# Keys and values of the last key tile as whole fp32 matmuls instead of three matmuls on parts

## What is computed

```python
# layer 0
memory_proj = einsum('bme,de->bmd', ctx, W_mem)
attn = softmax(einsum('bnd,bmd->bnm', x, memory_proj) / sqrt(256))
memory_context = einsum('bnm,bmd->bnd', attn, memory_proj)
gate = sigmoid(concat([x, memory_context]) @ W_gate.T + b_gate)
x = rmsnorm(x + gate * memory_context) * norm_w
# layer 1: 16 heads of 64
q = layernorm(x) @ Wq / 8
k, v = split(ctx @ Wkv)                 # (4, 512, 1024) each
sim = where(mask, q @ k.T, min)
x = x + tanh(attn_gate) * (softmax(sim) @ v) @ Wo
x = x + tanh(ff_gate) * gelu(layernorm(x) @ W1) @ W2
```

## Time and profile before

| | us |
|---|---|
| median of 3 runs | 209.27 |
| lowest, highest | 209.02, 211.89 |
| the profiled execution, its time | 210.25 |
| the profiled execution, its span in the trace | 208.4 |
| PE busy | 202.4 (97% of the span) |
| DVE busy | 148.0 (71%) |
| ACT busy | 130.5 (63%) |
| POOL busy | 71.3 (34%) |

### The profile page before, as it was taken

One profiled execution on the slowest core, in us unless ns is written; L12 is line 12 of the kernel. 1 busy time (PEld: TensorE's weight loads), 2 busy tenths in 40 slices (PEclk: granted clock), 3 DMA queues, 4 the chain that ended last, 5 costly groups with the idle time before them and its releaser, 6 DMA issues.

```text
span 208.4 us, 4502 instructions
## 1 busy us (share of the span) xinstructions
PE 202.4 (97%) x1505; PEld 169.1 (81%) x1505; DVE 148.0 (71%) x529; ACT 130.5 (63%) x414; POOL 71.3 (34%) x71
## 2 busy tenths in 40 slices
PE   7999999999999999999999999999999999999993
PEld 3567868888689799787978988888886799988992
DVE  1779997779967698778698889997479673235310
ACT  4386757849766787665665838979996820168300
POOL 2010423853336244407140664685725006000000
PEclk9999999999999999999999999999999999999999
DMA  6995060050000000000000000015000001100001
GB/s 184 301 378 193 5 203 0 5 201 0 0 3 2 3 2 0 5 2 3 0 2 3 0 2 3 0 32 174 2 0 3 0 0 34 48 25 0 24 32 58
DMA packets 9297, 10.06 MB, mean 48 GB/s; under 512 B 1330, under 2 KB 8116, under 8 KB 9268
## 3 DMA queue, kind: packets, MB, share of 16 engines
q1 hardware_dynamic: 8468, 9.32, 13.4%
q10 hardware_dynamic: 800, 0.39, 0.6%
HBM read 8.66 MB, written 1.05 MB: 47 GB/s over the span
## 4 chain that ended last, share of the span: by engine, by line
PE 90%; DMA 4%; DVE 2%; SPq 2%; issue 0%
PE bank L513 57%; PE bank L1338 9%; PE bank L1310 8%; PE bank L1452 8%; DMA ctx_sb<-in_ctx_dram 4%; PE bank L1348 3%; PE bank L1293 2%; PE bank L1378 2%; SPq L560 2%; PE bank L1218 1%; PE bank L1231 1%; DVE wkv_lo L1069 1%; DVE x_sb L1171 0%; PE bank L1364 0%; DVE ctx_probsT_even L1014 0%
## 5 line engine op out<-in xcount | busy, mean ns | idle before, releaser
L630 POOL TENSOR_TENSOR probs<-expd,row_rcp 128x512 f32<-128x512 f32 x39 | 40.2, 1050 | 54.4 <-DVE row_rcp L1004 49.7
L760 ACT ACTIVATE expd<-expd,neg_max 128x128 f32<-128x128 f32 x128 | 49.6, 392 | 2.4 <-DVE neg_max L994 2.4
L994 DVE CUSTOM_DVE_ANT_0 expd<-bank,mask_bias 128x128 f32<-128x128 f32 x128 | 28.2, 286 | 2.2 <-PE bank L1310 2.1
L513 PE MATMUL bank<-xhT_pair,wq_pair 128*128 128x256 f32 x192 | 26.1, 289 | 0.0
L513 PE MATMUL bank<-wo_pair,oT_pair 128*128 128x256 f32 x192 | 26.0, 288 | 0.0
L513 PEld LDWEIGHTS bank<-xhT_pair,wq_pair 128*128 128x128 f32 x192 | 23.8, 191 | 2.0 <-issue 1.2
L760 ACT ACTIVATION_READ_ACCUMULATOR expd<-expd,neg_max 128x1 f32 x128 | 24.5, 191 | 0.0
L513 PEld LDWEIGHTS bank<-wo_pair,oT_pair 128*128 128x128 f32 x192 | 23.9, 190 | 0.5 <-issue 0.4
L513 PE MATMUL bank<-wq_pair,gelu_pair 128*128 128x256 f32 x192 | 23.6, 284 | 0.1
L513 PEld LDWEIGHTS bank<-wq_pair,gelu_pair 128*128 128x128 f32 x192 | 23.3, 192 | 0.5 <-DVE x_sb L1171 0.4
L1338 PE MATMUL bank<-ident,probs 128*128 128x128 f32 x160 | 21.1, 275 | 0.0
(11 more groups left out here) (163 smaller groups left out, 358.5 us busy)
## 6 DMA issues: line engine op xcount, KB each, us to landing
stage<-in_L_xattn_W_dram SPq DMA_DIRECT2D x2, 1024.0 KB, 5.2
x_sb<-in_x_dram SPq DMA_DIRECT2D x4, 256.0 KB, 6.4
wkv_sb<-in_L_xattn_Wkv_dram SPq DMA_DIRECT2D x2, 512.0 KB, 6.2
stage<-in_L_xattn_Wq_dram SPq DMA_DIRECT2D x1, 1024.0 KB, 9.9
stage<-in_L_xattn_Wo_dram SPq DMA_DIRECT2D x1, 1024.0 KB, 5.3
out_dram<-x_sb SPq DMA_DIRECT2D x8, 128.0 KB, 1.8
ctx_sb<-in_ctx_dram SPq DMA_DIRECT2D x4, 192.0 KB, 6.6
probs<-in_L_xattn_W_gate_dram SPq DMA_DIRECT2D x1, 512.0 KB, 9.0
```

What stands on the lines that cost most here:

```text
L513: last = nc.tensor.matmul(bank_ap, lhs(a), rhs(c), start=start and n == 0, stop=stop and n == 2)
L630: nc.gpsimd.tensor_tensor(probs[:, r, :].rearrange("p (h k) -> p h k", h=hb), expd[:, r, :].rearrange("p (h k) -> p h k", h=hb), row_rcp[: ...
L760: last = nc.scalar.activation(here, here, ACT.Exp, bias=neg_max[:, r, h:h + 1], scale=-1.0, accum_out=row_sum[:, r, h:h + 1])
L994: last = nc.vector.tensor_tensor_reduce(expd[:, r, h * w:(h + 1) * w], SC[n % 2][:, h * w:(h + 1) * w], mask_bias[:, first:first + w], -1. ...
```

## The change

All 14 hot products that were made on parts (8 of keys, 6 of values) become one fp32 matmul each, straight from `wkv_sb` and `ctxT`. The stages `hotpair`, `splitk` and `splitv` leave the lists of ACT, DVE and POOL, with their tiles, semaphores and the wait of `splito` for the last key product. `TENSOR_ORDER` is unchanged, and in the short path the three other lists lose those stages and keep the order of the rest. `GENERAL_BEGIN` is written in a new order, for the path that these inputs don't take.

```diff
-    ("wmem",), ("xT", 0), ("xpair",), ("y", 0), ("branch", "ACT"), ("exp", "ctx", 0, 0), ("hotpair",),
-    ("v", "hot", 0, 0), ("splitk",), ("spread", "ctx", 0, 0), ("weights",), ("u", 0), ("gatemem",), ("splitq", 0),
-    ("k", "hot", 0), ("xT", 1), ("splitv",), ("splitq", 1), ("gate", 0), ("fuse", 0), ("k", "hot", 1),
...
+    ("wmem",), ("xT", 0), ("xpair",), ("y", 0), ("branch", "ACT"), ("exp", "ctx", 0, 0), ("v", "hot", 0, 0),
+    ("spread", "ctx", 0, 0), ("weights",), ("u", 0), ("gatemem",), ("splitq", 0), ("k", "hot", 0), ("xT", 1),
+    ("splitq", 1), ("gate", 0), ("fuse", 0), ("k", "hot", 1), ("k", "hot", 2), ("y", 1), ("v", "hot", 0, 1),
...
-        hot_keys = ctxT[:, :, HOT * P:M]
...
-                        nc.scalar.copy(key_weights(HI, half) if kind == "splitk" else value_hi[:, :], wkv_sb[:, half]
-                                       ).then_inc(act["kvhi"], 1)
...
-                        nc.scalar.copy(hot_pair[HI][:, :, :], hot_keys).then_inc(act["hot"], 1)
...
-                        if path.nt == 1:
-                            sc.wait_ge(pe["k"], PAIRS)
...
                     elif kind == "k":
                         b, pair = st[1:]
-                        if b == "hot":
-                            if c == 1:
-                                te.wait_ge(dve["kvlo"], 1)
-                                te.wait_ge(dve["hot"], 1)
-                            free(path, st)
-                            cols = slice(pair * P, (pair + 1) * P)
-                            split_matmul(path.bank(st)[:, :].rearrange("p (s n) -> p s n", s=KT),
-                                         lambda a: key_weights(a, cols), lambda a: hot_pair[a][:, :, :], True, True
-                                         ).then_inc(pe["k"], 1)
-                            continue
                         if c == 1:
                             te.wait_ge(w_in["wkey"], 16)
-                            te.wait_ge(dve["ctxT"], B + 1)
+                            te.wait_ge(dve["ctxT"], path.hot_keys_in() if b == "hot" else B + 1)
                         free(path, st)
-                        nc.tensor.matmul(path.bank(st)[:, :], wkv_sb[:, pair * P:(pair + 1) * P], ctxT[:, b, :],
-                                         start=True, stop=True).then_inc(pe["k"], 1)
+                        keys = ctxT[:, :, HOT * P:M] if b == "hot" else ctxT[:, b, :]
+                        nc.tensor.matmul(
+                            path.bank(st)[:, :].rearrange("p (s n) -> p s n", s=KT) if b == "hot"
+                            else path.bank(st)[:, :],
+                            wkv_sb[:, pair * P:(pair + 1) * P], keys, start=True, stop=True).then_inc(pe["k"], 1)
```

More of the change, by code:

```diff
@@ L82 @@
[L82 to L91, removed]
@@ new lines @@
+    ("splitq", 1), ("gate", 0), ("fuse", 0), ("k", "hot", 1), ("k", "hot", 2), ("y", 1), ("v", "hot", 0, 1),
+    ("v", "hot", 1, 0), ("k", "hot", 3), ("k", "hot", 4), ("exp", "ctx", 1, 0), ("v", "hot", 1, 1),
+    ("v", "hot", 2, 0), ("xhT", 0), ("rms", 0), ("rms", 1), ("rms", 2), ("rms", 3), ("spread", "ctx", 1, 0),
+    ("xT", 2), ("k", "hot", 5), ("k", "hot", 6), ("k", "hot", 7), ("splito", 0), ("mask",), ("u", 1), ("splito", 1),
+    ("exp", "head", 0, 0), ("gate", 1), ("exp", "head", 0, 1), ("spread", "head", 0, 0), ("fuse", 1),
@@ L105 @@
     ("scores", "ctx", 0, 0), ("norm", "ctx", 0, 0), ("v", "hot", 0, 0), ("v", "hot", 0, 1), ("ctxT", 1),
[L106 to L129, removed]
@@ L130 @@
-    ("x2hat", 1), ("split1", 1), ("q", 3, 3), ("norm", "head", 3, 1), ("scores", "head", 3, 2), ("av", 2, 3),
-    ("spread", "head", 3, 0), ("scores", "head", 3, 3), ("norm", "head", 3, 2), ("h2T", 0, 1), ("wo", 2, 0),
[5 rows of a table removed]
+    ("spread", "ctx", 0, 0), ("weights",), ("u", 0), ("lnq",), ("gatemem",), ("ctxT", 2), ("splitq", 0),
+    ("k", "hot", 0), ("k", "hot", 1), ("xT", 1), ("gate", 0), ("splitq", 1), ("rms", 0), ("scores", "ctx", 1, 0),
+    ("k", "hot", 2), ("k", "hot", 3), ("xhat", 0), ("norm", "ctx", 1, 0), ("v", "hot", 1, 0), ("v", "hot", 1, 1),
@@ new lines @@
+    ("k", "hot", 4), ("k", "hot", 5), ("xhT", 0), ("spread", "ctx", 1, 0), ("xT", 2), ("q", 0, 0), ("k", "hot", 6),
+    ("k", "hot", 7), ("u", 1), ("scores", "head", 0, 0), ("q", 0, 1), ("q", 0, 2), ("norm", "head", 0, 0),
+    ("scores", "head", 0, 1), ("gate", 1), ("scores", "head", 0, 2), ("norm", "head", 0, 1), ("q", 0, 3),
+    ("spread", "head", 0, 0), ("v", "hot", 2, 0), ("v", "hot", 2, 1), ("rms", 1), ("scores", "head", 0, 3),
+    ("xhat", 1), ("norm", "head", 0, 2), ("av", 0, 0), ("ctxT", 3), ("spread", "head", 0, 1), ("xhT", 1),
@@ new lines @@
+    ("scores", "ctx", 2, 0), ("norm", "head", 0, 3), ("q", 1, 0), ("av", 0, 1), ("q", 1, 1),
+    ("spread", "head", 0, 2), ("norm", "ctx", 2, 0), ("q", 1, 2), ("spread", "head", 0, 3),
+    ("scores", "head", 1, 0), ("spread", "ctx", 2, 0), ("norm", "head", 1, 0), ("scores", "head", 1, 1), ("u", 2),
+    ("xT", 3), ("scores", "head", 1, 2), ("norm", "head", 1, 1), ("av", 0, 2), ("gate", 2), ("rms", 2),
+    ("spread", "head", 1, 0), ("q", 1, 3), ("xhat", 2), ("norm", "head", 1, 2), ("av", 0, 3), ("xhT", 2),
@@ new lines @@
+    ("spread", "head", 1, 1), ("av", 1, 0), ("scores", "head", 1, 3), ("q", 2, 0), ("scores", "ctx", 3, 0),
+    ("norm", "head", 1, 3), ("norm", "ctx", 3, 0), ("wo", 0, 0), ("wo", 0, 1), ("wo", 0, 2), ("wo", 0, 3),
+    ("spread", "head", 1, 2), ("q", 2, 2), ("scores", "head", 2, 0), ("spread", "head", 1, 3), ("q", 2, 1),
+    ("av", 1, 1), ("spread", "ctx", 3, 0), ("v", "hot", 3, 0), ("v", "hot", 3, 1), ("norm", "head", 2, 0),
+    ("scores", "head", 2, 1), ("u", 3), ("ln2", 0), ("av", 1, 2), ("scores", "head", 2, 2), ("gate", 3), ("rms", 3),
@@ L137 @@
+    ("h2T", 0, 0), ("x2hat", 1), ("split1", 1), ("q", 3, 3), ("norm", "head", 3, 1), ("scores", "head", 3, 2),
+    ("av", 2, 3), ("spread", "head", 3, 0), ("scores", "head", 3, 3), ("norm", "head", 3, 2), ("h2T", 0, 1),
[5 rows of a table added]
     ("h2T", 1, 1), ("ff2", 0, 3), ("ff1", 1, 0), ("ff1", 1, 1), ("ff1", 1, 2), ("ff1", 1, 3), ("ff1", 1, 4),
@@ L142 @@
 POOL_ORDER = (
[L143 to L144 removed]
+    ("branch", "POOL"), ("norm", "ctx", 0, 0), ("rms", 0), ("norm", "ctx", 1, 0), ("splito", 0), ("splito", 1),
+    ("xhat", 0), ("norm", "head", 0, 0), ("norm", "head", 0, 1), ("rms", 1), ("norm", "head", 0, 2),
     ("norm", "head", 0, 3), ("norm", "ctx", 2, 0), ("norm", "head", 1, 0), ("xhat", 1), ("norm", "head", 1, 1),
@@ L156 @@
 GENERAL_BEGIN = (
[L157 to L161, removed]
+    ("any",), ("xT", 0), ("flag",), ("wmem",), ("ctxT", 0), ("tiles",), ("y", 0), ("ctxT", "hot"),
+    ("scores", "ctx", 0, 0), ("xpair",), ("exp", "ctx", 0, 0), ("norm", "ctx", 0, 0), ("ctxT", 1), ("weights",),
+    ("spread", "ctx", 0, 0), ("xT", 1), ("gatemem",), ("splitq", 0), ("lnq",), ("ctxT", 2), ("y", 1), ("u", 0),
+    ("scores", "ctx", 1, 0), ("splitq", 1), ("exp", "ctx", 1, 0), ("norm", "ctx", 1, 0), ("gate", 0), ("fuse", 0),
+    ("rms", 0), ("splito", 0), ("xhat", 0), ("mask",), ("xhT", 0), ("splito", 1), ("ctxT", 3), ("q", 0, 0),
 )
@@ L1410, in run @@
                         if c == 1:
                             te.wait_ge(w_in["wvalue"], 16)
-                            te.wait_ge(dve["ctxT"], path.at[("ctxT", 0)] if b == "hot" else B + 1)
+                        if b != "hot":
+                            te.wait_ge(dve["ctxT"], B + 1)
+                        else:
+                            te.wait_ge(dve["ctxT"], path.hot_keys_in() if s else path.at[("ctxT", 0)])
                         free(path, st)
-                        keys = ctxT[:, 0, HOT * P:M] if b == "hot" else ctxT[:, b, s * P:(s + 1) * P]
+                        keys = ctxT[:, s, HOT * P:M] if b == "hot" else ctxT[:, b, s * P:(s + 1) * P]
```

70 lines of the change are left out of this document (22 added, 48 removed), and 11 rows, old and new, of tables (SCALAR_ORDER, VECTOR_ORDER).

## The result

The changed kernel takes 210.86 us in the median of 20 runs, the kernel before 209.75 in 20 runs of the same comparison; the ratio is 1.0053, 95% interval 1.0035 to 1.0071.

What follows compares the result with a forecast made beforehand. PE, busy for 97% of the span, was taken to bound the kernel. 2.24 - 0.39 - 0.75 - 0.10 = +1.0 us, so 210.3 us on the median of 209.27, range 209.4 to 211.5.

Steps and rivals of the forecast that it cites:

- The price of a product: On PE, a whole product takes 0.86 us against 0.70 on parts; 14 x 0.16 = +2.24 us.
- The upper bound of 1.02: Span of a whole product's two records on PE, taken as highest possible price; 14 x 0.32 = 4.5 us.
- A product at two plain matmuls, 0.47 us: Rival from the skill page's half rate: the change saves 3.3 us, giving 206.0 us; chance 0.01.
- The first key product: It no longer waits for `wkv_lo`: 0.49 us regained, some 0.1 lost again at `gate`; credit -0.39 us.
- The stretch of keys and values: Three PE waits for DVE before the first query product (0.25 + 0.24 + 0.26) vanish as PE arrives later; credit -0.75 us.
- no weight load of it that waits for DVE: Sign in the profile after: the first query product, at 35.0 to 35.1 us, has no weight load waiting for DVE.
- DVE behind POOL: DVE's operation on `fused` falls from 1.07 to 0.42 us without POOL's subtraction; DVE wins 0.65, PE nothing by itself.
- Later: The 0.14 us gap at 50.53, behind a value product, is mostly covered by the product's extra 0.16; credit -0.10 us.
- PE's busy time: Sign in the profile after: PE's busy time up by about 2 us.
- the waits move along: Rival: DVE stays behind by as much as PE, the 0.75 credit is lost; +1.75, 211.0 us; chance 0.17.
- a product costs more than 0.86: Rival: drain or broken moving operand raises the price; at 1.02 each +3.2, 212.5 us; chance 0.08.
- the relief would outweigh the matmuls: Rival: the stretch to 35 us hangs on DVE's chain; 209.3 us; chance 0.04 faster, 0.09 no change to +0.5 us.

Runs made afterwards that it cites:

- e5: The changed kernel with each of the 14 hot products issued twice, the second over the first; ratio to the kernel before 1.0602, distance 200.12 us (+12.84).
- e8: The kernel before with only the first key product whole, ACT's copy of it ahead of its query-weight cast, and e7's move; ratio 1.0017, distance +0.40 us.
- e3: The kernel before without hotpair, splitk and splitv, hot products still three fp32r matmuls but on other existing tiles; ratio 1.0012, distance -0.13 us against before.
- e4: The changed kernel with hotpair, splitk and splitv still run at their old places, their parts unread by PE; ratio to before 1.0062, distance +1.12 us.
- e1: The kernel before with only the 8 key products whole and splitk dropped, the 6 value products on parts; ratio 1.0037, distance +0.55 us against before.
- e7: The kernel before with the copy of the fourth key product made by ACT instead of DVE; ratio 1.0001, distance +0.20 us against before.

## Why the prediction was right, step by step

**The price of a product** (0.86 against 0.70, from two pieces of the chain) holds: 0.86 in the chain after, 0.85 per copy in e5. The upper bound of 1.02 is the span of the same two records and not a price, and the strided operand of the key products costs nothing: keys and values are 0.86 alike. A product at two plain matmuls, 0.47 us, is refuted by the same rows. The Trainium skill, Perfetto Trace Analysis, section Engine Utilization, has the half rate that this reading came from; the rows don't give it for the product, and for each of its two records only nearly (0.43 us against 0.234, a factor of 1.84).

**The first key product.** The 0.49 us of credit were there. That `gate` would give 0.1 back held (0.08), though one of the two causes named was wrong. The copy of the first product and `bgate_parts` end within 0.06 us of each other in the changed kernel, and either could hold the load at 19.83:

```profile
19.10 0.57 ACT L775 COPY k_sb<-bank 128x512 f32<-128x512 f32 x1
```

```profile
19.14 0.47 DVE L923 SCALAR_TENSOR_TENSOR bgate_parts<-bgate_hi,ident,xhat 2x256 fp32r<-2x256 f32 x1
...
22.77 0.42 DVE L990 SCALAR_TENSOR_TENSOR fused<-fused,x_sb 128x256 f32<-128x256 f32 x1
...
29.66 0.68 DVE L1038 COPY k_sb<-bank 128x512 f32<-128x512 f32 x1
...
33.96 0.69 DVE L1031 TENSOR_TENSOR xhT_pair<-q_in,xhT_pair 128x512 fp32r<-128x512 f32 x1 [0.76 <-ACT xhT_pair L770]
```

```profile
19.83 0.53 PEld L504 LDWEIGHTS bank<-gate_mem_pair,uT_pair 128*128 128x128 f32 x3 [0.64 <-issue]
...
34.70 1.57 PEld L504 LDWEIGHTS bank<-xhT_pair,wq_pair 128*128 128x128 f32 x12 [0.48 <-DVE xhT_pair L1031]
```

e8, which takes the copy out of question, leaves `bgate_parts` (in the rows above it ends at 19.61, and the load comes 0.22 later).

**The stretch of keys and values.** The credit of 0.75 us was had in full, and for the reason given: PE comes later than the releases. DVE's copy that frees the bank of `("v", "hot", 2, 0)` ends at 29.66 + 0.68 = 30.34, and PE reaches that product at 30.73; counted from `gatemem`, the copy moved by 0.56 us (0.5 to 0.6 forecast) and PE by 0.87 (0.89 forecast). e3 (relief without longer matmuls: all gaps stay) and e4 (longer matmuls without relief: no gap) tell the two causes apart. What I had wrong is how safe it was. The first query product's weight load still waits 0.48 us for `xhT_pair`, which is ready at 33.96 + 0.69 = 34.65, and starts at 34.70; PE's matmuls of the key product before it run until 35.06, and that cover is all that hides it. The sign "no weight load of it that waits for DVE" did not come true, and e1, where PE is only 0.57 us late and not 0.9, shows gaps open again. The relief that I called what keeps the credit safe was not needed: e4 has none and no gap.

**DVE behind POOL.** 0.42 us at 22.77 in place of 1.07, and nothing on PE hangs on it; e4 has 0.99 there and loses nothing for it. The Trainium skill, SBUF — State Buffer, section SBUF: two separate sides, lets a GpSimd operation and a VectorE one with two SBUF inputs lock each other out. The traces agree: 0.99 to 1.07 us in the five that have POOL's subtraction there (before, e1, e4, e7, e8), 0.42 or 0.43 in the five without.

**Later.** The gap at 50.5 closed, 0.17 us with the piece behind it for the 0.10 expected. The rest of the span moved as a whole, as forecast. The first query product was forecast at 35.0 to 35.1 us, from the row of its weight load at 34.32. That row is at 34.70 now; it is the piece in the chain that begins at 35.06, and the same piece began at 36.02 - 1.43 = 34.59 before. So the agreement in the absolute time is luck, by two different events; what was forecast as a move of 0.7 is 0.64 us in the chain, counted from `gatemem`. PE's busy time rose by 0.9 us and not by the 2 that I had named as a sign: the gaps that the longer products fill already counted as busy, as 18.07 of 18.10 us before shows, so that sign was badly chosen.

**The rivals.** That the waits move along (+1.75) is refuted by the chain after and by e4. That a product costs more than 0.86 is refuted by the chain after and by e5. That the relief would outweigh the matmuls is refuted by e3, which has the relief alone and gains 0.13 us. The steps for e1, e7 and e8, made in the course of the experiments from the same picture of DVE's chain, were too sure of how a wait shrinks when its cause moves: it held where PE came later by more than any release could, and failed where only one of several waits in a row was shortened.

## What to carry to other kernels

Where one engine is busy all the time, count what an edit does to that engine first: relieving three others of some 2 us each was worth 0.1 to 0.2 us, and 0.16 us more on each of 14 products cost 2.2, of which filled gaps and the shed wait of the first product gave 1.3 back. Small gaps on the bound engine are a credit for work that is added there, since the added work arrives after the release it would have waited for; but to shorten one wait of several in a row often only moves it to the next. Take a price from how long a run of such instructions holds the chain, not from the length of modelled records.

## What the hardware showed

A whole fp32 product of 128 by 128 by 512 holds PE for 0.86 us, in two records of 0.43, and three fp32r matmuls of the same shape for 0.70. The ratio is 1.23, so parts are the cheaper form here, where making them is hidden (e3).

The first weight load of `gate` follows the end of `bgate_parts` by 0.22 to 0.25 us in nine traces (all but e5, where PE itself comes later), while its distance from ACT's copy ranges from 0.16 to 0.82 us. The load at 30.01 us before follows the copy that it waited for by 0.06. Several waits stand ahead of the former; that they are what takes the time was not tried.
